# An attention core on one Trainium2 core: the second query group's probabilities turned by VectorE and by transfers instead of by TensorE

## The reference

```python
# x: (4, 1024, 128); 16 heads of 64; hidden 384; one layer of each:
x = x + 0.5 * ffn(_layernorm(x), w_gate, w_up, w_down)
x = x + attn(_layernorm(x), wq, wk, wv, wo)
x = x + 0.5 * ffn(_layernorm(x), w_gate, w_up, w_down)
# attn
q = apply_rotary_emb(q, cos, sin)
k = apply_rotary_emb(k, cos, sin)
scores = jnp.einsum('bhid,bhjd->bhij', q, k, preferred_element_type=jnp.float32) * scale
scores = jnp.where(causal, scores, -jnp.inf)
probs = jax.nn.softmax(scores, axis=-1).astype(x.dtype)
out = jnp.einsum('bhij,bhjd->bhid', probs, v, preferred_element_type=jnp.float32).astype(x.dtype)
out = out.transpose(0, 2, 1, 3).reshape(batch, seq_len, NUM_HEADS * HEAD_DIM)
out = jnp.einsum('btd,od->bto', out, wo, preferred_element_type=jnp.float32)
```

## Time and profile before

| | us |
|---|---|
| median of 3 runs | 1253.42 |
| lowest and highest | 1252.69, 1255.08 |
| the profiled execution | 1256.88 |
| its span in the profile | 1255.0 |

### The profile page before, as it was taken

The page is one execution under the profiler, slowest core; times in us unless marked ns, Lnnn a source line. Parts: engine busy times, 40 slices in busy tenths (PEclk is TensorE's granted clock), DMA queues, the critical chain, the costliest instruction groups (busy, mean ns, idle before and its releaser), DMA issues. The chain is left out here.

```text
span 1255.0 us, 26509 instructions
## 1 busy us (share of the span) xinstructions
PE 1220.6 (97%) x7264; PEld 845.1 (67%) x7264; DVE 734.1 (58%) x1790; ACT 892.1 (71%) x1945; POOL 401.6 (32%) x223
## 2 busy tenths in 40 slices
PE   7996999999999999999999999999999999999898
PEld 4554776767676767676767777676767676766465
DVE  5565656565656565656566666556555656564454
ACT  4764777777777777777777777677777777777574
POOL 3343423332323333333333332323332333330000
PEclk8997999999999999999999999999999999999999
DMA  6236556565554555555555555546555455543000
GB/s 253 85 120 161 135 127 164 129 170 128 153 143 128 138 144 142 133 142 141 138 139 140 153 128 141 156 119 170 128 157 140 131 138 146 135 101 78 11 35 33
DMA packets 118606, 164.84 MB, mean 131 GB/s; under 512 B 14384, under 2 KB 64432, under 8 KB 118448
## 3 DMA queue, kind: packets, MB, share of 16 engines
q1 hardware_dynamic: 118176, 163.70, 49.2%
q10 hardware_dynamic: 400, 0.79, 0.3%
HBM read 53.02 MB, written 10.75 MB: 51 GB/s over the span
## 5 line engine op out<-in xcount | busy, mean ns | idle before, releaser
L1017 DVE CUSTOM_DVE_ANT_0 probs<-wide,tri_mask 128x1024 f32<-128x1024 f32 (+7 forms) x512 | 382.4, 754 | 251.0 <-PE wide L733 247.5
L922 ACT ACTIVATE shared_a<-bank 128x512 f32<-128x512 f32 (+2 forms) x640 | 338.5, 550 | 165.5 <-PE bank L749 159.6
L911 ACT ACTIVATE probs<-probs,neg_max 128x1024 f32<-128x1024 f32 (+7 forms) x512 | 394.5, 772 | 84.3 <-DVE neg_max L1017 82.1
L749 PEld LDWEIGHTS bank<-ident,probs 128*128 128x128 f32 x2304 | 259.5, 140 | 132.2 <-issue 70.1
L153 POOL TENSOR_TENSOR rotated<-terms,cross 128x1024 f32<-128x1024 f32 x62 | 148.5, 2396 | 613.0 <-DVE cross L147 612.8
L749 PE MATMUL bank<-ident,probs 128*128 128x128 f32 x2304 | 343.5, 278 | 1.1 <-ACT shared_a L922 0.4
L766 PE MATMUL bank<-shared_a,v_cur 128*64 128x256 f32 (+3 forms) x1792 | 297.3, 453 | 0.0
L732 PE MATMUL wide<-k_hh,q_hl 128*128 128x512 f32 (+3 forms) x768 | 288.8, 378 | 7.7 <-DMA k_low<-parts 5.5
L733 PE MATMUL wide<-k_low,q_hl 128*128 128x512 f32 (+3 forms) x768 | 255.7, 345 | 0.0
L766 PEld LDWEIGHTS bank<-shared_a,v_cur 128*64 128x64 f32 x1792 | 108.8, 136 | 121.8 <-issue 85.2
L732 PEld LDWEIGHTS wide<-k_hh,q_hl 128*128 128x128 f32 x768 | 146.3, 191 | 36.3 <-issue 24.1
(11 more groups left out here) (143 smaller groups left out, 1235.6 us busy)
## 6 DMA issues: line engine op xcount, KB each, us to landing
q_hl<-parts SPq DMA_DIRECT2D x254, 128.0 KB, 2.7
k_hh<-parts SPq DMA_DIRECT2D x254, 128.0 KB, 2.7
v_cur<-shared_b SPq DMA_DIRECT2D x32, 512.0 KB, 4.3
inv_sum<-inv_scratch SPq DMA_DIRECT2D x128, 128.0 KB, 3.1
k_low<-parts SPq DMA_DIRECT2D x63, 256.0 KB, 4.2
xn_cur<-xn_scratch SPq DMA_DIRECT2D x15, 1024.0 KB, 6.6
w_qk<-w_scratch SPq DMA_DIRECT2D x32, 256.0 KB, 3.1
w_scratch<-first_w_parts SPq DMA_DIRECT2D x8, 512.0 KB, 3.1
```

The costliest lines, as they stand in the source:

```text
L749: last = nc.tensor.transpose(ring[at % 2][:, col:col + P], probs[g][:, h, OFFSET[g][r] + j * P:OFFSET[g][r] + (j + 1) * P], ident[:])
L911: nc.scalar.activation(own, own, ACT.Exp, bias=neg_max[g][:, col], scale=-1.0, accum_out=sums[g][:, col]).then_inc(probs_done, 1)
L922: nc.scalar.activation(turned[:, slot, to], ring[at % 2][:, 0:w * len(heads)], ACT.Copy).then_inc(ring_free[at % 2], signals)
L1017: nc.vector.tensor_tensor_reduce(out=part_of_probs(g, k), in0=wide_banks[k % 2][:, x0:x1], in1=tri_mask[:, SEQ - (x1 - x0):], scale=1.0, s ...
```

## The change

The first query group stays as it was, except that its units' places in the ring and in `turned` are others. In the second group no block is turned by TensorE and none is copied by ScalarE. VectorE writes the masked scores of a row so that keys 4c + b lie at quarter b, place c (four quarters, `second`). After the exponential VectorE turns every 32x32 block of a unit in place (8 instructions a pair). Then SyncE copies the four groups of 32 partitions, each to one quarter of `spread`: partition c, quarter b goes to partition 4c + b, so that consecutive keys lie on consecutive partitions. There are two sets, query blocks 4 and 5, and query blocks 2 and 3, of four transfers each. A transfer of the first set has 128 rows of 704 elements (2816 bytes), one of the second 128 rows of 448 (1792 bytes).

`times_v_second` reads `spread` in runs of 32 elements, at most two query blocks (256 queries) wide, in three steps. The queries of the second group come out in the order quarter, block, place, which `normalise` undoes. `second` and `spread` have one buffer each: VectorE writes a set of `second` when the last copy from it has landed.

The keys and queries of a pair are filled in 8 transfers of 256 KB with rows of 4096 bytes instead of 16 of 128 KB with rows of 2048. SyncE's order in a pair is new, and so is TensorE's, VectorE's and ScalarE's.

```diff
+def fill_qk_whole(queue, o, u, h):
+
+    for part in range(2):
+        to = slice(HEAD_DIM * part, HEAD_DIM * (part + 1))
+        queue.dma_start(o.q_hl[u][h][to, :].bitcast(F32), rows_of(o, h, part, slice(0, SEQ))).then_inc(o.filled_qk[u][0], 16)
+        queue.dma_start(o.k_hh[u][h][to, :].bitcast(F32), rows_of(o, 2 + h, 0, slice(0, SEQ))).then_inc(o.filled_qk[u][1], 16)
...
-        UNITS = [(h, r) for h in range(2) for r in (3, 2, 1, 0)]
-        NU = 2 * len(UNITS)
+        UNITS = [[(h, r) for h in range(2) for r in (3, 2, 1, 0)], [(h, r) for s in range(2) for h in range(2) for r in (3 - 2 * s, 2 - 2 * s)]]
+        NU = 16
         KEYS = [tiles[3] + 1 for tiles in TILES]
-        NK = sum(KEYS)
-        TURNS = [[(0, (0,)), (0, (1,)), (1, (0,)), (1, (1,))] + [(j, (0, 1)) for j in range(2, 8)],
-                 [(j, (h,)) for j in range(4) for h in range(2)] + [(4, (0, 1)), (5, (0, 1))]]
-        RING = [[0, 1, 2, 3, 4, 5, 7, 9, 10, 11], [12, 13, 14, 15, 16, 17, 18, 19, 21, 23]]
-        RING_SUM, RING_OUT = [6, 20], [22, 8]
-        NR = 24
-        N_QK, N_LOW = 16 * 8, 16 * 2
+        SECOND_STEPS = [(0, (0, 1, 2)), (0, (3, 4, 5)), (1, (0, 1, 2, 3))]
+        NK = KEYS[0] + len(SECOND_STEPS)
+        TURNS = [(0, (0,)), (0, (1,)), (1, (0,)), (1, (1,))] + [(j, (0, 1)) for j in range(2, 8)]
+        TURNED_AT = [0, 1024, 1792, 2304, 2816, 3328, 0, 512]
+        STEPS_BEFORE = [8 - NK, 2 - NK, 3 - NK, 4 - NK, 5 - NK, 6 - NK, 1, 1]
+        SET_ROWS = [(2, 3), (0, 1)]
+        SET_LEN = [HALF * sum(TILES[1][r] + 1 for r in rows) for rows in SET_ROWS]
+        QUARTERS = 4
+        RING = [0, 1, 2, 3, 4, 7, 8, 9, 10, 11]
+        RING_SUM, RING_OUT = [5, 12], [13, 6]
+        NR = 14
...
+        second = [sb(f"second{s}", [P, QUARTERS, 2 * SET_LEN[s]]) for s in range(2)]
+        spread = [sb(f"spread{s}", [P, QUARTERS, 2 * SET_LEN[s]]) for s in range(2)]
...
+        def part_of_second(k):
+            h, r = UNITS[1][k]
+            rows, n = SET_ROWS[k // 4], TILES[1][r] + 1
+            c0 = SET_LEN[k // 4] * h + (r - rows[0]) * HALF * (TILES[1][rows[0]] + 1)
+            return second[k // 4][:, :, c0:c0 + HALF * n]
...
+            def times_v_second(p, u, d):
+                s, blocks = SECOND_STEPS[d]
+                if d == 0:
+                    may_multiply(p, 1)
+                pe.wait_ge(spread_full[s], 16 * QUARTERS * (p + 1))
+                for j in blocks:
+                    rows = [r for r in SET_ROWS[s] if TILES[1][r] >= j]
+                    for h in range(2):
+                        out = out_bank[HEAD_DIM * h:HEAD_DIM * (h + 1), :].rearrange("p (a r i) -> p a r i", a=QUARTERS, r=4)
+                        out = out[:, :, rows[0], :] if len(rows) == 1 else out[:, :, rows[0]:rows[-1] + 1, :]
+                        last = nc.tensor.matmul(out, v_cur[:, u, j, HEAD_DIM * h:HEAD_DIM * (h + 1)], spread_of(s, h, j, rows),
+                                                start=(j == 0), stop=(j == TILES[1][SET_ROWS[s][1]]))
+                last.then_inc(out_step, 1)
...
+                own = part_of_second(k) if g == 1 else part_of_probs(k)
...
+                if k % 4 == 0 and g == 1 and some(p):
+                    dve.wait_ge(spread_full[k // 4], 16 * QUARTERS * p)
                 x0, x1 = scores_at(g, k)
+                own, scores, masked = part_of_probs(k) if g == 0 else None, wide_banks[k % 2][:, x0:x1], tri_mask[:, SEQ - (x1 - x0):]
+                if g == 1:
+                    own = part_of_second(k).rearrange("p b c -> p c b")
+                    scores, masked = (a.rearrange("p (c b) -> p c b", b=4) for a in (scores, masked))
                 settle(dve)
-                nc.vector.tensor_tensor_reduce(out=part_of_probs(g, k), in0=wide_banks[k % 2][:, x0:x1],
-                                               in1=tri_mask[:, SEQ - (x1 - x0):], scale=1.0, scalar=3e38, op0=ALU.add,
+                nc.vector.tensor_tensor_reduce(out=own, in0=scores, in1=masked, scale=1.0, scalar=3e38, op0=ALU.add,
                                                op1=ALU.min, accum_out=neg_max[g][:, col]).then_inc(scores_taken, 1)
 
-            def keep_turned(p, u, g, t, signals=1):
-                j, heads = TURNS[g][t]
-                at, w = RING[g][t], P * len(rows_at(g, j))
-                dve.wait_ge(ring_full, ring_count(p, at))
-                if some(NK * p + KEYS[0] * g + j - 3):
-                    dve.wait_ge(out_step, NK * p + KEYS[0] * g + j - 3)
-                slot = (NK * u + KEYS[0] * g + j) % 4
-                to = slice(heads[0] * w, (heads[-1] + 1) * w)
-                nc.vector.tensor_copy(turned[:, slot, to], ring[at % 2][:, 0:w * len(heads)]).then_inc(ring_free[at % 2], signals)
+            def turn_blocks(p, k):
+                dve.wait_ge(probs_done, unit(p, 1, k))
+                own = part_of_second(k)
+                nc.vector.transpose(own, own).then_inc(blocks_turned, 1)
...
+                if g == 0:
+                    nc.vector.tensor_tensor(head_out[:], out_bank[:], inv_sum[0][:], ALU.mult).then_inc(head_done, 1)
+                else:
+                    to, factor = (a[:].rearrange("p (r a i) -> p a r i", r=4, a=QUARTERS) for a in (head_out, inv_sum[1]))
+                    nc.vector.tensor_tensor(to, out_bank.rearrange("p (a r i) -> p a r i", a=QUARTERS, r=4), factor,
+                                            ALU.mult).then_inc(head_done, 1)
...
+            def send_second(p, s):
+                sp.wait_ge(blocks_turned, 8 * p + 4 * (s + 1))
+                if some(p):
+                    settle(sp)
+                    sp.wait_ge(out_step, NK * (p - 1) + (NK - 1, NK)[s])
+                for a in range(QUARTERS):
+                    sp.dma_start(spread[s][:, a, :], second[s][HALF * a:HALF * (a + 1), :, :]).then_inc(spread_full[s], 16)
...
+                next_qk()
+                send_inv(p, 0)
+                next_low()
+                spread_inv(p, 0)
+                next_v()
+                send_second(p, 0)
                 send_inv(p, 1)
+                next_inputs()
                 spread_inv(p, 1)
+                send_second(p, 1)
+                next_wo()
```

More of the change, by code:

```diff
@@ L1093, in pair @@
                 next_max(3)
+                turn_blocks(p, 7)
                 normalise(p, 0)
@@ L1207, in pair, with next_qk @@
-                if has_next and not (first and u == 0):
-                    may_fill(p + 1)
-                    for c in range(2):
+                has_next, later = not (last and u == 1), not (first and u == 0)
+                def next_qk():
+                    if has_next and later:
+                        may_fill(p + 1)
                         for h in range(2):
-                            fill_qk(sp, o, 1 - u, c, h)
-                send_inv(p, 0)
-                if has_next and not (first and u == 0):
-                    for h in range(2):
-                        fill_low(sp, o, 1 - u, h)
@@ L1216, in pair, with next_low @@
-                spread_inv(p, 0)
-                if has_next:
-                    copy_v(p + 1, i + u, 1 - u)
-                    if not (first and u == 0):
-                        sp.wait_ge(ring_full, ring_count(p, RING_OUT[1]))
-                    load_wo(1 - u, (2 * i + u + 1) % PAIRS)
-                    if not (last or (last is None and u == 1)):
+                            fill_qk_whole(sp, o, 1 - u, h)
+                def next_low():
+                    if has_next and later:
+                        for h in range(2):
+                            fill_low(sp, o, 1 - u, h)
```

225 lines of the change are left out of this document (114 added, 111 removed).

## The result

The changed kernel takes 1272.54 us (median of 4 runs, 1263.74 to 1280.22) against 1254.25 for the kernel before (4 runs, 1252.69 to 1255.71): a ratio of 1.0151, with an interval of 1.0117 to 1.0184. Every ratio is taken over the runs of a kernel that lie within 1.5% of its fastest, which leaves out two runs of `wide_source` and none of any other kernel. The profiled execution is the slowest of the four, 1280.22, with a span of 1278.5 us.

The account below looks back on a forecast made before the run. The DMA queue was to replace TensorE as the bound at 33.1 us a pair against 32.5: 28 pairs +17 us, three pairs -11, last transfer +3, giving 1262 us against the 1253.4 median; range 1215 to 1305 us (wider range 1160 to 1325).

Parts of the forecast that it names:

- TensorE, removed and added: TensorE per pair: 36 turned blocks go, 4.0 us; narrower value products add 0.3 us; 28.8 us would remain.
- The bounds for run-wise reads: TensorE's reads and PSUM writes in runs of 32 elements: taken at nothing, bounds nothing and 2.3 us.
- The length of a pair before: Spacing of the 64 output projections in the kernel before: 63 intervals, 31.5 pairs, 32.5 us a pair.
- VectorE's transposes: Eight VectorE transposes of 4608 columns a pair: 6.0 us, at 0.15 us plus 1.05 ns a column.
- VectorE's strided writes: VectorE's second-group masked scores, 4608 columns with a stride: taken as free, at most 4.8 us more a pair.
- The queue's work: DMA queue per pair: 21.0 us of transfers plus 11.6 for the new ones at 204 GB/s, 32.6 us.
- Latency in the queue: SyncE's wait for the second group's sums, sent behind four `spread` transfers: a mean of 0.5 us a pair left uncovered.
- The queue comes to it later: First `spread` set is ready at VectorE's fourth transpose, some 14 us in; the queue first does 18 us of other transfers.
- The 3.7 us that TensorE saved are spent there: TensorE spends its saved 3.7 us a pair waiting before the first product that reads the late-landing `spread`.
- The ends: First pairs and last two run at TensorE's pace: three pairs x 3.7, -11 us; last pair's open transfer wait, +3.
- The fast queue: Rival: DMA queue faster, TensorE stays the bound, 29.0 to 30.0 us a pair, 1161 us; chance 0.23.
- VectorE in the way: Rival: strided writes at two cycles keep VectorE busy 30.4 us; some 34 us a pair, 1290 us; chance 0.13.

Follow-up runs that it names:

- wide_source: Changed kernel with each `spread` transfer reading one row from each of 128 partitions instead of four from 32, keys in wrong order: median 1233.74 us, ratio 0.9756.
- both_off: Changed kernel with the second group's masked scores in natural order and only a quarter of each `spread` row copied: 1143.43 us, ratio 0.9112.
- plain_max: Changed kernel with the second group's masked scores written in natural order, without VectorE's stride, keys in another order than the values: 1256.16 us, ratio 1.0018.
- v_by_gpsimd: Changed kernel with `v_cur` copied by GpSimd instead of by a transfer on SyncE's queue, same result: 1270.72 us, ratio 1.0135.
- order_by_need: Changed kernel with GpSimd copying `v_cur`, `spread` transfers ordered 0, 2, 1, 3, VectorE's fourth transpose before three strided maxima, ScalarE's unit-3 exponential before a copy: 1250.11 us.

## Why the prediction came out as it did

The forecast was 1262 us with the queue as the bound, and the time is 1272.5, slower as forecast and inside the forecast's own range. That it came so near was luck in part. The prediction called the sign nearly open, and its sum got there with errors that partly cancel: the queue's own work was 3.4 us a pair too high, the time in which it stands still 3.9 us too low, and the pair before 0.6 us too low.

- *TensorE, removed and added*: right. 1152 turned blocks are left, and `both_off` shows 29.6 us a pair where 29.4 should be left. The bounds for run-wise reads were not needed.
- *The length of a pair before*: it was too low. It came from all 63 intervals between projections, whose last are short; in the loop a pair took 33.1 us. All per-pair figures of before are 2% short for that.
- *VectorE's transposes*: right to 20 ns at 768 and 384 columns.
- *VectorE's strided writes*: the term that was mis-sized. Taken as free, they cost 561 + 487 + 378 + 295 ns for the four widths between after and `plain_max`, and twice that a pair: 3.4 us, inside the bounds of nothing and 4.8. The stride of the written rows was the one access with no row behind it, and "free" was the wrong end to take. From 384 to 768 columns a strided write takes (1514 - 831)/384 = 1.78 ns a column. The Trainium skill's rule that the prediction named for this rival holds, and a second page of the skill has its price, which the prediction missed: "Vector Engine (DVE) Microarchitecture Reference", on the SBUF access granule, gives 1.71 ns a column where the output hops at every element and 1.054 where it doesn't. By it, an estimate, the term is 4608 x 0.66 = 3.0 us a pair. The trace agrees within 0.4 us.
- *The queue's work*: right in its bytes (209 GB/s x 33.6 us = 7.0 MB a pair), too high in its time. The new transfers take 512 x 208 ns and 512 x 117 ns over 16 engines, 10.4 us and not 11.6, and the share of 0.87 is 29.2 us of the pair and not 32.6.
- *Latency in the queue*: forecast at 0.5 us, and 4.4 us of a pair are not filled. "The queue comes to it later" is the step that failed: the queue was at the first `spread` set before VectorE's fourth transpose, since that came 16.7 us behind the first fill (603.91 to 620.6), with the dearer maxima in front of it (in `plain_max`, without them, SyncE's wait for the transposes is 7.6 us in all instead of 45.7), and what was to be moved before it was less than the forecast's 18 us. `v_by_gpsimd` fits this: it takes from the queue just before that point, and gains nothing. The forecast's other wait, for the sums to land, was priced for the second group alone; in after it is 106.5 us in all, of both groups, and more than twice the wait for the transposes.
- *Where TensorE waits*: "The 3.7 us that TensorE saved are spent there", in front of the first product that reads `spread`, did not come true as such. Those waits are 26.5/32 = 0.8 us a pair, those for `xn_cur` 1.1, those for VectorE 1.3, and the lower clock, which the prediction did not count, some 0.7.
- *The ends*: the 11 us that three pairs at TensorE's pace were to save are not there. The first four pairs took 34.7 us each instead of 33.1 (+6.5), the 22 after them +10.5 in all, and the rest of the span +6.5: the profiled difference of 23.5 us.
- *The fast queue* (1161): wrong, and the Trainium skill's fabric figure for SBUF to SBUF ("DMA: Bandwidth & Descriptors") does not hold for a source of 32 partitions; `wide_source` shows that it is the source. 16 packets of 2816 bytes in 208 ns are 217 GB/s. The Trainium skill's "SBUF — State Buffer" gives 218 GB/s as the asymptote for 32 partitions, in the section on the DMA port swizzle, and the measurement agrees; the prediction's 204 was 6% low. *VectorE in the way* (1290, 34 us a pair) was a part of what happened; it had 0.13. The two were priced as rivals, and the truth was both, in turn.

Of what would show the steps: the DMA share near 0.9 with 7.0 MB at 210 GB/s and the projections' distance came true, and TensorE's idle in front of `spread` in part; the maxima "the same by their width" did not.

## What to carry to other kernels

An access with a step of 16 bytes or more was not free here, on VectorE or on TensorE, and layout work moved from one engine to the next takes its price along: price it from a row before it is counted as hidden. Where two resources hand over to each other inside a loop, a sum per resource is only a lower bound; look for the stretch in which one is full and the other stands still. Moving the instruction that releases the hand-over gave 0.7% here and cost no work; taking work from both resources gave 4.2%. For the length of a loop's turn, compare instructions with the same place in it.

## What the runs showed of the hardware

- VectorE, 768 columns of float32 into another layout: 953 ns with runs, 1514 with writes of neighbours 2816 bytes apart, 1539 with reads 16 bytes apart.
- TensorE, moving float32 columns 16 bytes apart: 0.94 ns a column against 0.45.
- A copy from SBUF to SBUF with rows of 2816 bytes: 208 ns a packet on average from 32 partitions, 116 ns from 128, with rows as long; the medians are 112 and 113 ns.
- Fills of 256 KB and of 128 KB in a full queue: 1272.5 and 1272.2 us for the kernel.
- TensorE's granted clock was 0.75 and 0.68 in the two stretches of three us around a wait of 2.24 us, and 1.00 again from 608 us on; from 440 to 770 us its mean was 0.98, and 1.00 in `order_by_need`, where that kind of wait is gone.
